# A macaron block on one Trainium2 core: the FFN's output turned back by VectorE and two DMAs instead of TensorE, and the first chunk in another order

## What is computed

```
def ffn(x):                                  # x: tokens by 128
    shared = silu(x @ Ws_up) @ Ws_down       # 128 -> 64 -> 128
    aff = x @ centroids.T                    # tokens by 64 experts
    _, idx = top_k(aff + expert_biases, 8)
    w = sigmoid(aff[idx]); w = w / (sum(w) + 1e-08)
    cw = scatter(w, idx)                     # tokens by 64, eight of them not zero
    h = silu(einsum('td,edf->etf', x, W_up))
    y = einsum('etf,efd->etd', h, W_down)
    return shared + einsum('etd,te->td', y, cw)

x = x + 0.5 * ffn(layernorm(x))
q, k, v = layernorm(x) @ Wq.T, @ Wk.T, @ Wv.T
x = x + softmax(q @ k.T) / sqrt(128) @ v
x = x + 0.5 * ffn(layernorm(x))
```

## Time and profile before

| | us |
|---|---|
| median of three runs | 539.09 (538.56 to 539.78) |
| the profiled execution | 538.72 |
| its span | 536.9 |
| TensorE busy in the span | 529.3 |
| VectorE busy | 410.5 |
| ScalarE busy | 404.4 |
| GpSimd busy | 273.9 |

### The profile page before, as it was taken

The page is one execution under the profiler, slowest core; times in us unless marked ns, Lnnn a source line. Parts: engine busy times, 40 slices in busy tenths (PEclk is TensorE's granted clock), DMA queues, the critical chain, the costliest instruction groups (busy, mean ns, idle before and its releaser), DMA issues.

```text
span 536.9 us, 8686 instructions
## 1 busy us (share of the span) xinstructions
PE 529.3 (99%) x2686; PEld 434.6 (81%) x2686; DVE 410.5 (76%) x939; ACT 404.4 (75%) x809; POOL 273.9 (51%) x242
## 2 busy tenths in 40 slices
PE   7999999999999999999999999999999999999997
PEld 6577887887788888799999999878887888788886
DVE  5999689877976677867777889779768867975664
ACT  6898778777877775866667657778779777877773
POOL 3689757775776764000000000267676776766663
PEclk9999999999999999999999999999999999999999
DMA  7667555554556650000000000165565565666652
GB/s 256 199 215 211 169 199 167 163 195 174 171 175 189 203 167 1 2 0 1 1 2 2 0 1 1 45 193 170 164 204 169 167 194 181 183 175 190 206 193 84
DMA packets 50318, 72.25 MB, mean 135 GB/s; under 512 B 15296, under 2 KB 16064, under 8 KB 50272
## 3 DMA queue, kind: packets, MB, share of 16 engines
q1 hardware_dynamic: 49616, 71.17, 42.1%
q10 hardware_dynamic: 592, 0.39, 0.3%
q0 software_dynamic: 64, 0.13, 0.1%
HBM read 69.57 MB, written 2.10 MB: 133 GB/s over the span
## 4 chain that ended last, share of the span: by engine, by line
PE 91%; DVE 3%; ACT 3%; DMA 1%; issue 1%; SPq 0%; POOL 0%; DVEq 0%
PE lrow L1191 13%; PE lrow L1192 13%; PE lrow L1193 13%; PE bank L1233 11%; PE bank L1235 10%; PE bank L1234 10%; PE bank L1296 5%; PE bank L1511 3%; PE bank L1513 3%; PE bank L1512 3%; DMA raw<-in_w_up 1%; PE bank L1303 1%; DVE pmax L975 1%; PE bank L1192 1%; PE bank L1193 1%
## 5 line engine op out<-in xcount | busy, mean ns | idle before, releaser
L301 POOL TENSOR_TENSOR gpart_lo<-gated,gpart_hi 128x512 fp32r<-128x512 f32 x174 | 223.8, 1296 | 160.2 <-ACT gpart_hi L474 158.5
L463 ACT ACTIVATE lrow<-lrow 128x512 f32<-128x512 f32 (+1 forms) x245 | 143.9, 587 | 61.3 <-PE lrow L1193 60.8
L728 DVE TENSOR_TENSOR gated<-lrow,wide 128x512 f32<-128x512 f32 x170 | 116.1, 683 | 51.0 <-ACT lrow L463 49.9
L474 ACT CAST gpart_hi<-gated 128x512 fp32r<-128x512 f32 x174 | 106.7, 613 | 6.7 <-DVE gated L728 6.1
L1233 PE MATMUL bank<-gpart_lo,wdn_hi 128*128 128x512 f32 x246 | 97.8, 398 | 0.0
L1235 PE MATMUL bank<-gpart_hi,wdn_hi 128*128 128x512 f32 x246 | 97.5, 396 | 0.0
L1234 PE MATMUL bank<-gpart_hi,wdn_lo 128*128 128x512 f32 x246 | 97.1, 395 | 0.0
L728 DVE TENSOR_TENSOR lrow<-lrow,wide 128x512 f32<-128x512 f32 x74 | 51.5, 695 | 28.1 <-ACT lrow L463 26.4
L1109 DVE TENSOR_TENSOR pT_lo<-bank,pT_hi 128x512 fp32r<-128x512 f32 x64 | 43.7, 684 | 21.7 <-ACT pT_hi L660 21.5
L301 DVE TENSOR_TENSOR gpart_lo<-lrow,gpart_hi 128x512 fp32r<-128x512 f32 (+1 forms) x83 | 56.6, 682 | 1.6 <-ACT gpart_hi L474 1.3
L660 ACT CAST pT_hi<-bank 128x512 fp32r<-128x512 f32 x64 | 38.1, 595 | 24.0 <-PE bank L1296 23.8
(11 more groups left out here) (280 smaller groups left out, 970.8 us busy)
## 6 DMA issues: line engine op xcount, KB each, us to landing
wide<-gates_dram SPq DMA_DIRECT2D x488, 128.0 KB, 3.0
raw<-in_w_up SPq DMA_DIRECT2D x8, 256.0 KB, 6.3
raw<-in_w_down SPq DMA_DIRECT2D x8, 256.0 KB, 6.5
x<-in_x SPq DMA_DIRECT2D x3, 256.0 KB, 4.1
gates_dram<-gate_blocks SPq DMA_DIRECT2D x24, 32.0 KB, 2.0
out_dram<-x SPq DMA_DIRECT2D x3, 256.0 KB, 3.0
gates_dram<-gates SPq DMA_DIRECT2D x2, 128.0 KB, 2.3
x<-in_x SPq DMA_DIRECT2D x1, 128.0 KB, 2.7
```

The costliest lines, as they stand in the source:

```text
L301: return eng.tensor_tensor(gpart[1][0:m, U % NGP, :], gated_at(U)[0:m, :], gpart[0][0:m, U % NGP, :].bitcast(F32), ALU.subtract)
L463: nc.scalar.activation(dst[0:m, :], hid[U % NH][0:m, :], ACT.Silu).then_inc(s_silu, 1)
L474: nc.scalar.copy(gpart[0][0:m, U % NGP, :], gated_at(U)[0:m, :]).then_inc(s_ghi, 1)
L728: nc.vector.tensor_tensor(gated_at(U), a, b, ALU.mult).then_inc(s_gated, 1)
```

## The change

Six chunks (0, 1, 2, 4, 5, 6) get another way from yT to x. In the next chunk VectorE turns the PSUM sum in 32x32 blocks into `y_blocks` (`y_turned`, unit 7), SP stores these by four DMAs to DRAM ahead of the gate loads of units 14 to 17, so that the blocks come to their places, and loads them by tokens ahead of unit 20 (`load_y`). At unit 18 VectorE adds half of them to x, both operands in SBUF. `epi_y` and `epi_yT` are gone. The first FFN's stats go from unit 10 to 19, their root from 12 to 20, `normed(1, ...)` from 20 and 21 to 22 and 23, the turn to kT from 26 to 27.

In the first chunk, the routing's bank is halved so that VectorE starts on two tiles while TensorE does the other two; `cwT` is copied in halves and the gates after it, behind `hi_unit(1)`; GpSimd makes one of the small high parts and leaves its second weight piece until the gates are made; three weight loads (wv, wq, wk) go from ScalarE's and GpSimd's queues to SP's, ahead of unit 31's gates. In every chunk the 1e-8 of the gate sum becomes a 65th column, so that one small operation falls out.

```
+            def store_y(n, b):
+
+                sp.wait_ge(e_y, n + 1)
+                rows = y_d.rearrange("(k t) (b d) -> b t k d", t=SQ, d=SQ)
+                sp.dma_start(rows[b], y_blocks[b * SQ:(b + 1) * SQ, :].rearrange("t (k d) -> t k d", d=SQ)).then_inc(s_yout, 16)
+
+            def load_y(n):
+
+                sp.wait_ge(s_yout, 16 * (P // SQ) * (moves(n) + 1))
+                sp.dma_start(y_tok[:, :, :], y_d.rearrange("(i p) d -> p i d", p=P)).then_inc(s_ytok, 16)
...
+                    if n == 0 and u == 31:
+                        sp.dma_start(raws[:, E + F:LOADED], wv_d).then_inc(s_value, 16)
+                        for i, src in enumerate((wq_d, wk_d)):
+                            sp.dma_start(raw_qk[:, i * D:(i + 1) * D], src).then_inc(s_qk, 16)
...
+                    if 14 <= u < 18 and n % NCH:
+                        store_y(n - 1, u - 14)
+                    if u == 20 and n % NCH:
+                        load_y(n - 1)
...
-                        for k in range(PRE):
+                        piece_lo(0)
+                        pool.wait_ge(p_cw, 1)
+                        for k in range(1, PRE):
                             piece_lo(k)
...
-                        if f == 0 and c and u == 12:
+                        if f == 0 and c and u == 20:
                             rstd(1, c - 1, e_st, e_rs)
...
-            def epi_y(n):
-                act.wait_ge(s_down, place(PAIRS, n) + 1)
                 if n:
-                    act.wait_ge(e_yT, n)
-                nc.scalar.mul(yT[:, :], yacc[n % 2][:, :], 0.5).then_inc(e_y, 1)
...
+                            for h in range(2):
+                                act.wait_ge((f_cwT, p_cwT)[h], 1)
+                                nc.scalar.copy(cwT[:, h * GW:(h + 1) * GW], (mp, bank[0])[h][:, 0:GW]).then_inc((f_cwr, p_cwr)[h], 1)
                             piece_hi(2)
+                            silu_unit(3, n)
+                            hi_unit(1, n)
                             pro_cwT(n)
-                            silu_unit(3, n)
...
-                link(nc.vector.tensor_reduce(total, rec[:, :, :], AX, ALU.add))
-                link(nc.vector.tensor_scalar(wsum[:, 0, :], total, 1e-8, None, ALU.add))
-                nc.vector.reciprocal(inverse_sum(n), wsum[:, 0, :]).then_inc(p_inv, 1)
+                link(nc.vector.tensor_reduce(total, rec_guard[:, :, :], AX, ALU.add))
+                nc.vector.reciprocal(inverse_sum(n), total).then_inc(p_inv, 1)
...
+            def y_turned(n):
+
+                dve.wait_ge(s_down, place(PAIRS, n) + 1)
+                nc.vector.transpose(y_blocks[:, :], yacc[n % 2][:, :]).then_inc(e_y, 1)
+
             def epi_x(n, c):
-                dve.wait_ge(e_yT, n + 1)
-                nc.vector.tensor_tensor(x[:, c * TPC:(c + 1) * TPC, :], x[:, c * TPC:(c + 1) * TPC, :],
-                                        mq[:, :].rearrange("p (t d) -> p t d", d=D), ALU.add).then_inc(e_x, 1)
+
+                dve.wait_ge(s_ytok, 16 * (n - n // NCH + 1))
+                nc.vector.scalar_tensor_tensor(out=x[:, c * TPC:(c + 1) * TPC, :], in0=y_tok[:, :, :], scalar=0.5,
+                                               in1=x[:, c * TPC:(c + 1) * TPC, :], op0=ALU.mult, op1=ALU.add).then_inc(e_x, 1)
...
-                            if u == 9:
+                            if u == 7:
+                                y_turned(n - 1)
+                            if u == 18:
                                 epi_x(n - 1, c - 1)
                             if f == 0:
-                                if u == 10:
+                                if u == 19:
                                     epi_stats(c - 1)
-                                if u == 20:
+                                if u == 22:
                                     if c > 1:
                                         dve.wait_ge(e_v, c - 1)
                                     normed(1, c - 1, c - 1, xn2, e_rs, e_xn, (0, 1))
...
-            def epi_yT(n):
-                pe.wait_ge(e_y, n + 1)
```

More of the change, by code:

```diff
@@ L133, in macaron_kernel @@
         yT = sb("yT", [P, CH], F32, ffn)
+        y_blocks, y_tok = sb("y_blocks", [P, CH], F32, ffn), sb("y_tok", [P, TPC, D], F32, ffn)
         xn2 = sb("xn2", [P, TPC, D], F32, ffn)
@@ L433, in _ @@
                             low_part(nc.gpsimd, place(u, n)).then_inc(s_glop, 1)
+                        if n == 0 and u == 0:
+                            rstd(0, 1, p_st, p_rs)
                         if n == 0 and u % 2 == 0 and PRE + u // 2 < 2 * WP:
@@ L436, in _ @@
                         if c + 1 < NCH:
-                            if u == 3:
+                            if n and u == 3:
                                 rstd(0, n + 1, p_st, p_rs)
@@ L507, in pro_cwT @@
                     act.wait_ge(s_gout, stored(n - 1))
-                nc.scalar.copy(gates[:, :], mp[0:E, :]).then_inc(s_gates, 1)
-            def epi_y(n):
-                act.wait_ge(s_down, place(PAIRS, n) + 1)
                 if n:
-                    act.wait_ge(e_yT, n)
-                nc.scalar.mul(yT[:, :], yacc[n % 2][:, :], 0.5).then_inc(e_y, 1)
+                    nc.scalar.copy(gates[:, :], mp[0:E, :]).then_inc(s_gates, 1)
+                else:
+                    nc.scalar.copy(gates[:, 0:GW], mp[0:E, 0:GW])
+                    nc.scalar.copy(gates[:, GW:CH], bank[0][0:E, 0:GW]).then_inc(s_gates, 1)
             def last_y(n):
                 act.wait_ge(s_down, place(UNITS - LAG - 1, n) + 1)
-                act.wait_ge(e_yT, n)
+                if n // NCH:
+                    act.wait_ge(e_yT, n // NCH)
                 nc.scalar.mul(yT[:, :], yacc[1][:, :], 0.5).then_inc(h_ya, 1)
@@ L619, in _ @@
                         if c:
-                            if u == LAG + 1:
-                                epi_y(n - 1)
-                            if f == 0 and u == 27:
+                            if f == 0 and u == 28:
                                 epi_hi(c - 1)
-                            if n == 1 and u == 31:
+                            if n == 1 and u == 32:
                                 epi_proj_hi(0)
@@ L891, in first_top @@
                 dve.wait_ge(s_bias, 16)
-                dve.wait_ge(p_aff, 1)
-                nc.vector.tensor_tensor(b[:, :, :], bank[0][:, 0:TPC * E].rearrange("p (t e) -> p t e", e=E),
-                                        bc(bias[:, :]), ALU.add).then_inc(f_bias, 1)
-                dve.wait_ge(f_bias, 1)
-                for i in range(TPC):
-                    ins = nc.vector.max(top[:, i, :], b[:, i, :])
+                for h in range(2):
+                    some = slice(h * GT, (h + 1) * GT)
+                    dve.wait_ge((f_aff, p_aff)[h], 1)
+                    nc.vector.tensor_tensor(b[:, some, :], (bank[0], mp)[h][:, 0:GT * E].rearrange("p (t e) -> p t e", e=E),
+                                            bias[:, :].unsqueeze(1).to_broadcast([P, GT, E]), ALU.add).then_inc(f_bias, 1)
+                    dve.wait_ge(f_bias, h + 1)
+                    for i in range(h * GT, (h + 1) * GT):
+                        ins = nc.vector.max(top[:, i, :], b[:, i, :])
                 ins.then_inc(p_max, 1)
@@ L1219, in spread_gate @@
                     one = sel[:, u - 1, :, :].rearrange("p e f -> p (e f)")
+                    if n == 0 and u == 1:
+                        for h in range(2):
+                            pe.wait_ge((f_cwr, p_cwr)[h], 1)
+                            half = slice(h * GW, (h + 1) * GW)
+                            ins = nc.tensor.matmul(gate_bank(u, n)[:, half], one, cwT[:, half], start=True, stop=True)
+                        ins.then_inc(s_gate, 1)
+                        return
                     nc.tensor.matmul(gate_bank(u, n), one, cwT[:, :], start=True, stop=True).then_inc(s_gate, 1)
@@ L1320, in pro_cw @@
                 pe.wait_ge(p_cw, n + 1)
-                turn(flat(cw2), mp, p_cwT)
-            def epi_yT(n):
-                pe.wait_ge(e_y, n + 1)
-                pe.wait_ge(j_lo, joint(n + 1))
-                if 0 < n < NCH:
-                    pe.wait_ge(e_prlo, 1)
-                    pe.wait_ge(e_lo, n)
-                elif n == 0:
-                    pe.wait_ge(w_Alo, 1)
-                else:
-                    pe.wait_ge(e_x, n)
-                turn(yT, mq, e_yT)
+                if n == 0:
+                    for i in range(TPC):
+                        h, at = i // GT, i % GT * P
+                        ins = nc.tensor.transpose((mp, bank[0])[h][:, at:at + P], flat(cw2)[:, i * P:(i + 1) * P], ident[:, :])
+                        if i % GT == GT - 1:
+                            ins.then_inc((f_cwT, p_cwT)[h], 1)
+                else:
+                    turn(flat(cw2), mp, p_cwT)
             def epi_xT(c):
@@ L1398, in first_aff @@
                     pe.wait_ge((f_lo, p_lo)[i // GT], 1)
```

(6 more changed lines are left out.)

85 lines of the change are left out of this document (53 added, 32 removed).

## The result

The changed kernel takes 547.53 us at the median of four runs (546.96 to 549.5), beside 538.94 for the kernel before: a ratio of 1.0163, 95% interval 1.0147 to 1.0178. It is slower, as forecast, but by 8.6 us instead of 5, and outside the range. The profiled execution took 546.96, 8.24 more than that of before.

A forecast was written before the change was run, and what follows sets the result against it. TensorE was taken to bound the kernel, other engines counting only where they make it wait. Terms −2.3 + 4.8 + 1.4 + 0.4 + 1.0 − 0.2 gave +5.1 on the profiled 538.72; forecast median 544.0 us, range 537.0 to 546.5.

The forecast's parts named there:

- the term for chunks 5, 6 and 7: Add, port wait and loads there, but 3.15 us of VectorE idle and no stats: +0.4 for the three (0 to 2.2).
- the port wait: VectorE's add, with two SBUF operands, waits for GpSimd's current low part: +0.5 in chunk 2's reckoning.
- The turn: Four transposes of yT leave TensorE in six chunks, 0.38 us each: −2.3.
- The stretch of chunks 1 and 2: Units 18 to 20: added add and stats, waits for port and root, less VectorE's lead and idle time: +2.4 each.
- rival C: GpSimd goes first at the port, so the add in chunks 1, 2, 5 and 6 waits longer: up to +3.0, 547; chance 0.07.
- Chunk 3's 1.6 for 1.4: Stores in SP's queue of gate loads make the load of y late for VectorE: +1.4 (0 to 2.2).
- The border's 1.5 for 1.0: Chunks 0 to 1: three weight loads on SP ahead of unit 31's gates make late gates later: +1.0 (0.7 to 1.4).
- The first chunk: Gate 1 comes 0.7 to 1.7 earlier, but most is lost at unit 12 to later gate loads: −0.2 (−0.7 to +0.5).
- The VectorE turn: 128x512 transpose at unit 7, taking between 0.68 and twice that, regained two units later: taken as zero.
- Rival A: VectorE's lead absorbs add, stats and waits, chunk 3's load is in time, the border's cost goes: 537.0; chance 0.2.
- B: Only lower bounds: no port wait, no wait for the root, chunk 3's load in time: +0.5, 539.6; chance 0.13.
- D: Chunk 0's loads hold and the first chunk gives its 1.7: 542.5; within the forecast's range, sharing its 0.6 chance.

The follow-up runs named there:

- weights_mid: Changed kernel with wv, wq and wk loaded by SP ahead of unit 22's gates of chunk 0 and the gates' copy straight behind cwT's: 546.63 us.
- weights_back: Changed kernel with the wv, wq and wk loads at the program's start again, on ScalarE's and GpSimd's queues: 547.34 us.
- root_earlier: Changed kernel with GpSimd's root of the attention's stats ahead of unit 20's low part instead of behind it: 542.26 us.
- y_on_act: Changed kernel with y's four stores (units 10 to 13) and load (unit 16) issued by ScalarE instead of SP: 546.76 us.
- best3: best2 with the four stores of y in chunks 3 and 7 issued by ScalarE (units 10 to 13): 535.11 us.
- late_all: Changed kernel with add at unit 24 (26 in second FFN), stats and root 25, norm 27 and 28, kT turn 29, weight loads at start, gates' copy early: 539.18 us.
- mended: Changed kernel with root ahead of unit 20's low part, second-FFN add at unit 26, three weight loads at start, gates' copy straight behind cwT's: 538.66 us.
- no_y: Changed kernel with the y path as before the change; first chunk's rework, weight loads on SP and 65th column stay: 538.53 us.
- best2: late_all with the kT turn at unit 31, first wqk product in the next chunk, three weight loads on SP behind the first weight pieces: 536.23 us.
- late_add: Changed kernel with the add of y to x at unit 26 instead of 18 in the second FFN (chunks 5 to 7): 545.87 us.
- one_wide: Changed kernel with one 256 KB gate load of two rows for each unit instead of two of 128 KB: 1453.73 us.

## Why the prediction was wrong

**The step that failed** is the term for chunks 5, 6 and 7, that they "have the add, the port wait and the loads, but 3.15 us of VectorE idle in the stretch", and so +0.4 for the three. They cost 4.1: 0.3, 0.3 and 3.5. I put chunk 7 with 5 and 6 by VectorE's idle time. It belongs with chunk 3, by SP's queue. SP in chunk 7 of the kernel before, from 490 to 512:

```profile
489.88 22.32 SPq L365 DMA_DIRECT2D wide<-gates_dram  x34
```

These are 34 issues without a gap, 0.66 each, two for every unit of 1.40: a row like the one that I read for chunk 3 in the earlier trace rows, and there I had drawn the conclusion that the load of y comes late. That SP's issues and the place of the add make chunk 7's loss is seen across the profiles. With chunk 7 as in the changed kernel it loses 3.5, 3.6 (weights_mid), 2.2 (weights_back) and 1.5 (root_earlier). With the add at unit 26 it loses 0.6 to 1.3 in five kernels, and with the stores on ScalarE 0.4 (y_on_act) and nothing (best3). In chunks 5 and 6 the idle time did not save the add either: it waited for GpSimd in one and for the load in the other, 0.3 each.

**What I had no term for** is the clock. A stall in my sum cost its own length; in chunk 7 the fall behind it cost 1.6 more. The same fall stands in the profiles of weights_mid (the first two rows, chunks 1 and 7) and weights_back (chunk 2); the granted clock is the third number from the end:

```profile
104.00:106.00 2.00, 2.00 (x8) 1.46 (x7) 1.45 (x4) 1.66 (x3) 2.00 (x2) 0.54 0.33 81
...
521.00:523.00 2.00, 2.00 (x7) 1.52 (x6) 1.26 (x3) 1.48 (x3) 1.76 (x2) 0.50 0.70 212
...
156.00:158.00 2.00, 2.00 (x8) 1.62 (x8) 1.29 (x2) 1.09 (x2) 1.92 (x4) 0.50 0.49 121
```

**The rest, term by term.** The turn gave 2.74 for my 2.3, so 0.46 each where the step in the earlier trace rows is 0.38; the runs don't show what the other 0.08 is.

The stretch of chunks 1 and 2 came out at 2.4 and 2.5 for 2.4 each. In chunk 2 it was by the waits that I had named: 0.5 for the add behind GpSimd's low part, 0.9 for the root. In chunk 1 the root's 0.9 was there, but not the port wait; in its place the load of y came 0.38 late, where I had said that it lands before unit 18, so part of that agreement is luck. root_earlier and late_all show that it is the root and this place. In chunk 2 the add went in ahead of `weights`, so rival C is out. The Trainium skill's page "SBUF — State Buffer" (section "SBUF: two separate sides") has the port held for a whole instruction, and this trace agrees, with 0.5 us lost by the add and then 0.4 by `weights`.

Chunk 3's 1.6 for 1.4 is luck too. VectorE waited 1.62 for y_tok, as I had it, and 0.97 for the root as well, which I had not counted there. root_earlier, with y_tok still 0.87 late, loses only 0.25 in chunk 3; y_on_act, with y_tok 0.81 late and the root as it was, loses 1.3. So about 1.0 of the 1.6 is the root's and 0.4 the load's.

The border's 1.5 for 1.0 lies just past its upper bound of 1.4. The first chunk: 1.6 gained and lost again, as I said, but at units 16 to 18 instead of 12. The VectorE turn takes 0.71, near the lower bound, and is hidden. Rival A is out: the stalls of chunks 1 to 3 and the border are 8.1, far over the 2.1 from which it would have decided. B is out, as its waits came, and D, as the first chunk's gain was lost.

The range was wrong apart from this. It is called one by the bounds of the terms, but these add up to −0.7 at the lower end (−1.7 with D's first chunk) and +9.4 at the upper, which makes 548.5 as a median; 546.5 comes from no sum of them. The 547.53 would lie inside the wider range, by luck, since the term for chunks 5 to 7 lies outside its own bound of 2.2.

Three things stay open: why the border still loses 1.1 to 1.5 with the loads ahead of unit 22's gates (one store of the gate blocks then took 1.4 and 1.9 us to issue instead of 0.6, and no row says what it waited for) and 0.8 in mended; why chunk 7's stall is shorter in root_earlier; and what sets the drift in the second FFN.

## What to carry to other kernels

When a step moves to a DMA queue, count that queue's issues per unit of work against the unit's time, and do it for every chunk, since chunks differ. In chunk 7 SP needed 1.3 of 1.4 us, and five more issues came out as late loads and a stall. A result that crosses two engines (stats, root, norm) wants its middle step ahead of the long operation on the slower engine: one line's move took 5.3 us off here, 3.3 of it where the root had been waited for.

Where the operations of the y path stand decides what it costs: from the changed kernel to best3 the time falls from 1.6% over the kernel before to 0.7% under it. That the y path itself is then a gain is not shown, since no kernel has best3's first chunk and weight loads without it. From unit 7 of chunk 1 to the end best3 gains 2.2 on the kernel before in its profile, no_y 1.5 and best2 1.1, so the y path comes to between a gain of 0.7 and a loss of 0.4, by one profile of each.

## What the runs showed of the hardware that was not expected

The profiles of the changed kernel, y_on_act, late_add, weights_back and weights_mid have 13 stalls of TensorE of 1.9 to 2.1 us. Behind four of them its granted clock fell to the lower level, and each fall cost about 1.6 us. Length alone does not decide: in the changed kernel the clock fell behind the 1.86 of chunk 7 and not behind the 2.05 and 2.08 of chunks 1 and 2, and no row shows what does. Behind stalls of 1.4 or less it fell in none of the profiles. By the mean granted clock, executions of one kernel differ as well: 0.989 to 1.0 in weights_back.

An issue on SP took 5.0 us at the median in one_wide, where two engines carried each load, and 0.6 in the changed kernel. That SP then waits for the transfers is argued from these two, and no row names what it waited for. ScalarE issued the stores of y in 0.31 each in best3, SP in 0.58 in the changed kernel.
